# A linear-attention and mixture-of-experts layer: x loaded a second time in turned layout, and a new place for the normalisation of x1

## The chip, the cores and the metric

The kernel runs on one core of a Trainium2 chip. The metric is the time on the device in microseconds (us); less is better. TensorE is called PE here as in the profile (PEld is its weight load), VectorE is DVE, ScalarE is ACT, GpSimd is POOL and SyncE, which here only issues DMAs, is SP.

## The reference

x has 8 batches of 512 tokens with 256 features, in float32. One layer is two blocks, each with a residual and a layer norm:

```
q, k, v = x@Wq+bq, x@Wk+bk, x@Wv+bv         # 16 heads of 16 features
q, k = elu(q)+1, elu(k)+1
kv = sum over tokens of k v^T, per head and batch
attn = q @ kv;  gate = sigmoid(x@Wg+bg)
x1 = layernorm(x + (gate*attn)@Wo + bo)
weights, experts = top 4 of softmax(x1@gate_w.T), from the best 2 of 4 groups
y = sum over the 4 experts of weight * (silu(x1@w1)*(x1@w3))@w2
z = (silu(x1@ws1)*(x1@ws3))@ws2              # shared expert
out = layernorm(x1 + y + z)
```

## The kernel before

The program is written out by hand for each engine's queue; nothing plans it. It has four stages. First the attention of the eight batches, in a loop of batches (`batch(b, ...)` exists once for each engine). Then the shared expert for three batches. Then the routed experts in two waves of 48 blocks of 256 token rows each: the rows of x1 are sent by indirect DMAs of POOL into a table in HBM sorted by expert, SP loads blocks of it, PE turns and multiplies them, and SP stores the results. Last, POOL gathers the results and DVE adds them up and normalises, while PE does the shared expert for the other batches.

A product of float32 quality is made of three products of 16-bit halves: every operand is split in a high part by ACT (a copy to float16, `xt_hi`, `split_hi`) and a low part by DVE (a subtraction, `xt_lo`, `split_lo`).

In the attention of batch b, PE does in this order: `project_kv` of four token tiles (with `project_out(b - 1)` after the second), the transposes of the next batch's x (`transpose_x(x_in, ...)`), the two halves of q, the transposes of x1 of batch b - 1 (`transpose_x(x_all[...])`), the first half of the gate g, `sum_kv`, the second half of g, the routing products of batch b - 1 (`count_tokens`, `route`), and `attend(b)`. The transposes of x and of x1 go into the same two PSUM banks (`t_bank`).

ACT takes k and v out of PSUM (`take_kv`), makes the high half of the next x (L500), normalises x1 (L510), evaluates relu and exp of q (`q_parts`, L554 and L557), makes the high half of x1 (L505), splits two experts' weights (L516, L517) and evaluates the gate (L569). In ACT's batches 2 to 5 such a split also stands between the second and third `take_kv`.

DVE applies the gate (L686), finishes the routing of batch b - 2 (`routing_tail`), adds the residual (L718), takes the statistics (L691, L699), makes the low half of the next x (L671), adds the bias bo to the next x (`x_plus_bias`, L704, from `x_in` to `x_all`), finishes k (L913), splits weights (L709), finishes q (L919), makes the low half of x1 (L677), masks kv (L927, L930) and starts the routing of batch b - 1 (L730). Its queue, like the others, runs strictly in order. POOL makes from mean and variance four small instructions (L426 to L431), the last being the shift of the layer norm, which ACT waits for.

SP loads x of batch b into `x_in` (L262) once `x_plus_bias` of the batch before has read it, and the experts' weights into `stage` (L268, L270) once the split before is done. Between two loads of weights it writes, three times over, four blocks of zeros of 512 KB to the table in HBM (L292), and then loads x. At the start it issues the load of x of batch 0, the attention's weights, biases and constants, the shared expert's weights, and then waits.

Of the kernel before, what the change touches and what calls it, by code (L numbers as in the profile page):

```python
# [16 lines left out]
P = 128  # L17
# [15 lines left out]
def attention_and_experts(nc: bass.Bass, x, Wq, bq, Wk, bk, Wv, bv, Wg, bg, Wo, bo,  # L33
                          gate_w, w1, w2, w3, ws1, ws2, ws3, plan_consts, out):
# [36 lines left out]
    with ExitStack() as ctx:  # L71
# [11 lines left out]
        x_in = sb("x_in", [P, TT, D])  # L83
# [16 lines left out]
        eps = sb("eps", [P, TT])  # L100
# [102 lines left out]
        x_loaded, wa_loaded, small_loaded = sem("x_loaded"), sem("wa_loaded"), sem("small_loaded")  # L203
# [14 lines left out]
        x_transposed, xt_hi_ready, xt_lo_ready = sem("x_transposed"), sem("xt_hi_ready"), sem("xt_lo_ready")  # L218
# [9 lines left out]
        bn_ready, mv_ready, rstd_ready = sem("bn_ready"), sem("mv_ready"), sem("rstd_ready")  # L228
        x1_ready, x1_transposed, rstd_step = sem("x1_ready"), sem("x1_transposed"), sem("rstd_step")
# [30 lines left out]
        def _(sp):  # L260
            def load_x(b):
                sp.dma_start(x_in[:, :, :], x[b].rearrange("(p t) d -> p t d", p=P)).then_inc(x_loaded, 16)  # L262
# [9 lines left out]
            load_x(0)  # L272
# [9 lines left out]
            load_stage(0)  # L282

# [15 lines left out]
            def next_x(b):  # L299
                sp.wait_ge(x_biased, b)  # L300
                load_x(b)
# [97 lines left out]
        def _(pool):  # L399
# [5 lines left out]
            pool.memset(eps[:, :], LN_EPS).then_inc(const_ready, 1)  # L405
# [15 lines left out]
            pool.wait_ge(const_ready, 6)  # L421
# [71 lines left out]
        def _(act):  # L493
# [39 lines left out]
            def batch(b, prev, prev2, nxt, early=None, mid=None):  # L533
# [11 lines left out]
                if prev:  # L545
# [915 lines left out]
```

## Time and profile before

| what | us |
|---|---|
| median of 3 runs | 700.07 |
| the three runs | 700.07, 696.46, 704.74 |
| the profiled execution, its own time | 707.36 |
| span of that execution | 705.5 |
| PE busy | 527.1 (75%) |
| DVE busy | 427.4 (61%) |
| ACT busy | 300.1 (43%) |
| POOL busy | 290.1 (41%) |
| mean granted PE clock | 0.916 |

The span is from the first to the last instruction of the profiled execution. Busy time is summed over instructions, and PE's weight loads overlap its products. Attention takes the first 227 us of the span, the shared expert the time to 270, the two waves of experts that to about 600, and the rest is gathering, adding and the last shared products. A release named "remote" is one for which the profile shows no sender.

### The profile page before, as it was taken

To read this page: it belongs to the slowest core of one execution; us is meant where nothing else is said; L and a number is where in the kernel's file an instruction comes from. 1 tells how busy PE (TensorE), PEld (TensorE's weight loads), DVE (VectorE), ACT (ScalarE), POOL (GpSimd) and SP (SyncE) were. 2 spreads that over 40 slices of the span, in tenths; PEclk is the share of its full clock that TensorE was granted. 3 is DMA by queue.
4 is the path that set the end of the run, shared out by engine and by line. 5 is a ranking of instruction groups with operands and counts; after the bars stand their busy time and mean duration, and the time that the engine had idled before them with its cause. 6 is when DMAs were issued, how large, how long until landed. Compare 5 with 4: busy or idle time off the path is not lost.

```text
span 705.5 us, 13461 instructions
## 1 busy us (share of the span) xinstructions
PE 527.1 (75%) x3532; PEld 357.0 (51%) x3555; DVE 427.4 (61%) x1200; ACT 300.1 (43%) x659; POOL 290.1 (41%) x334
## 2 busy tenths in 40 slices
PE   1899887889897688789786688798888779665400
PEld 1355443555544357567574566576667566421300
DVE  2447783776864866666554444377757556652784
ACT  2536653436524343555454555356546445110100
POOL 1000126456446402454444200644446251777574
PEclk9999997899999899999999999899999989977755
DMA  7022428295451303767767766687787753333332
GB/s 202 13 75 76 156 90 284 82 304 209 177 185 68 103 18 106 239 204 230 232 228 259 238 223 216 180 235 233 211 261 231 223 181 134 105 120 89 94 114 99
DMA packets 64091, 118.63 MB, mean 168 GB/s; under 512 B 9760, under 2 KB 23088, under 8 KB 64048
## 3 DMA queue, kind: packets, MB, share of 16 engines
q1 hardware_dynamic: 51216, 84.55, 37.1%
q0 software_dynamic: 12288, 33.57, 15.1%
q8 instruction: 19, 0.31, 0.2%
q14 instruction: 24, 0.20, 0.1%
q10 hardware_dynamic: 544, 0.00, 0.0%
HBM read 55.17 MB, written 62.91 MB: 167 GB/s over the span
## 4 chain that ended last, share of the span: by engine, by line
PE 36%; DVE 19%; issue 15%; SPq 9%; another core or an unknown queue 6%; ACT 6%; DMA 5%; POOL 4%; ACTq 0%; DVEq 0%; POOLq 0%
PE t L1340 4%; PE h_even L1149 4%; PE h_even L1151 4%; PE h_odd L1149 3%; PE h_even L1150 3%; PE h_odd L1151 3%; PE h_odd L1150 3%; DVE x_all L1055 2%; SPq L327 2%; PE y L1186 2%; DMA kv<-expert_in 2%; SPq L330 1%; PE y L1373 1%; SPq L334 1%
## 5 line engine op out<-in xcount | busy, mean ns | idle before, releaser
L440 POOL DMA_INDIRECT expert_in<-x_all,slots x128 | 132.9, 1038 | 117.8 <-PE h_odd L1151 45.0
L452 POOL DMA_INDIRECT wa_stage<-expert_out,result_of x64 | 62.9, 983 | 35.3 <-issue 18.1
L1340 PE MATMUL t<-ident,kv 128*128 128x128 f32 x384 | 60.3, 280 | 19.4 <-DMA kv<-expert_in 15.0
L452 POOL DMA_INDIRECT q_fm<-expert_out,result_of x32 | 32.4, 1014 | 85.6 <-DMA expert_out<-q_exp 63.9
L426 POOL TENSOR_SCALAR neg_mean<-mv 128x4 f32<-128x4 f32 x16 | 4.6, 290 | 149.5 <-DVE mv L699 149.3
L1044 DVE TENSOR_TENSOR wa_lo<-bias_heads,wa_hi 128x256 bf16<-128x256 f32 x96 | 40.5, 422 | 41.3 <-ACT wa_hi L642 30.1
L1149 PE MATMUL h_even<-xsT_hi,we_hi 128*128 128x256 f16 x192 | 54.3, 283 | 10.7 <-issue 8.8
L1340 PEld LDWEIGHTS t<-ident,kv 128*128 128x128 f32 x384 | 45.3, 145 | 26.8 <-DMA kv<-expert_in 12.1
L1025 DVE TENSOR_TENSOR xsT_lo<-t,xsT_hi 128x512 bf16<-128x512 f32 x72 | 49.5, 688 | 11.6 <-ACT xsT_hi L617 5.9
L1150 PE MATMUL h_even<-xsT_lo,we_hi 128*128 128x256 bf16 x192 | 54.2, 282 | 2.5 <-issue 2.5
L1151 PE MATMUL h_even<-xsT_hi,we_lo 128*128 128x256 f16 x192 | 54.2, 282 | 1.4 <-issue 1.4
L617 ACT ACTIVATE xsT_hi<-t 128x512 f16<-128x512 f32 x72 | 42.0, 585 | 16.6 <-PE t L1340 12.8
L642 ACT ACTIVATE wa_hi<-bias_heads 128x256 f16<-128x256 f32 x96 | 39.7, 414 | 20.7 <-DVE bias_heads L1036 14.4
L1036 DVE TENSOR_TENSOR bias_heads<-h_odd,kv_heads 128x256 f32<-128x256 f32 x48 | 20.2, 420 | 41.8 <-ACT kv_heads L634 40.9
L1036 DVE TENSOR_TENSOR bias_heads<-h_even,kv_heads 128x256 f32<-128x256 f32 x48 | 20.1, 419 | 34.4 <-ACT kv_heads L634 30.9
L634 ACT ACTIVATE kv_heads<-h_odd 128x256 f32<-128x256 f32 x48 | 18.3, 381 | 52.8 <-remote 25.0
L1186 PE MATMUL y<-wo_sb,gated 128*128 128x256 f32 x128 | 33.3, 419 | 9.3 <-DVE gated L686 9.3
L452 POOL DMA_INDIRECT gate<-expert_out,result_of x32 | 30.5, 954 | 19.4 <-PE h_even L1151 10.0
L529 ACT ACTIVATE kv<-h_even 128x256 f32<-128x256 f32 x32 | 12.3, 386 | 58.3 <-PE h_even L1151 52.4
L634 ACT ACTIVATE kv_heads<-h_even 128x256 f32<-128x256 f32 x48 | 18.2, 380 | 43.8 <-PE h_even L1151 17.4
L1367 PE MATMUL y<-we_hi,wa_hi 128*128 x96 | 26.8, 279 | 12.6 <-issue 10.7
L624 ACT ACTIVATE k_exp<-y 128x512 f32<-128x512 f32 x48 | 28.7, 598 | 15.9 <-PE y L1373 14.3
(222 smaller groups left out, 1530.0 us busy)
## 6 DMA issues: line engine op xcount, KB each, us to landing
kv<-expert_in SPq DMA_DIRECT2D x96, 256.0 KB
expert_out<-k_exp SPq DMA_DIRECT2D x48, 256.0 KB
expert_out<-q_exp SPq DMA_DIRECT2D x48, 256.0 KB
expert_in<-wa_stage SPq DMA_DIRECT2D x16, 512.0 KB
expert_in<-wa_stage SPq DMA_DIRECT2D x32, 256.0 KB
stage<-in_L_ffn_w SPq DMA_DIRECT2D x48, 128.0 KB
x_in<-in_L_attn_x SPq DMA_DIRECT2D x8, 512.0 KB
out<-gated SPq DMA_DIRECT2D x8, 512.0 KB
```

The costliest lines, as they stand in the source:

```text
L440: pool.indirect_dma_start(xs_dram[b // WB], bass.IndirectOffsetOnAxis(ap=slots[:, b, t, j:j + 1], axis=0), x_all[:, b, t, :], None).then_i ...
L452: pool.indirect_dma_start(y_got[i][:, j, :], None, ys_dram[w], bass.IndirectOffsetOnAxis(ap=result_of[:, b, t, j:j + 1], axis=0)).then_inc ...
L617: act.activation(xsT_hi[r][:, :, :], t_bank[r % 2][:, :].rearrange("p (c n) -> p c n", c=KC), ACT.Copy).then_inc(xst_hi_ready, 1)
L642: act.activation(aT_hi[r % 2][:, :], a_pair, ACT.Copy).then_inc(at_hi_ready, 1)
L1025: dve.tensor_tensor(xsT_lo[r][:, :, :], t_bank[r % 2][:, :].rearrange("p (c n) -> p c n", c=KC), xsT_hi[r][:, :, :], ALU.subtract).then_in ...
L1036: dve.tensor_tensor(a_pair, h_banks[r % 2][0][:, 2 * P:], s_pair, ALU.mult).then_inc(pair_a_ready, 1)
L1044: dve.tensor_tensor(aT_lo[r % 2][:, :], a_pair, aT_hi[r % 2][:, :], ALU.subtract).then_inc(at_lo_ready, 1)
L1149: pe.matmul(dst, sta_hi, mov_hi, start=start, stop=False)
L1150: pe.matmul(dst, sta_hi, mov_lo, start=False, stop=False)
L1151: return pe.matmul(dst, sta_lo, mov_hi, start=False, stop=stop)
L1186: last = pe.matmul(y_bank[h][:, (t % 2) * D:(t % 2 + 1) * D], gated[:, c, t * P:(t + 1) * P], wo_sb[:, c, :], start=c == 0, stop=c == KC - 1)
L1340: last = pe.transpose(t_bank[r % 2][:, c * 2 * P + i * P:c * 2 * P + (i + 1) * P], xs[r][:, i, c * P:(c + 1) * P], ident[:, :])
```

## The change

A second copy of x is passed in as `x_turned`, with features before tokens, so that a DMA loads it just as the products want it. SP loads it into `x_in` (`load_xt`) once the low half of the batch before is made, and loads x itself straight into `x_all` (`load_x`); DVE adds bo there in place. The transposes of x on PE go, ACT and DVE read `x_in` in place of the PSUM banks, and PE's order becomes q, first half of g, transposes of x1, `sum_kv`. ACT normalises x1 between the two halves of `q_parts`, and evaluates the gate's first half before it takes the transposed x1. DVE makes the negative mean (for the first layer norm only) and variance plus epsilon; POOL is left with the power, and with the shift in the first layer norm only.

```diff
+            def load_xt(b):
+                sp.dma_start(x_in[:, :, :], x_turned[b].rearrange("(c p) s -> p c s", p=P)).then_inc(xt_loaded, 16)
+
             def load_x(b):
-                sp.dma_start(x_in[:, :, :], x[b].rearrange("(p t) d -> p t d", p=P)).then_inc(x_loaded, 16)
+                sp.dma_start(x_all[:, b, :, :], x[b].rearrange("(p t) d -> p t d", p=P)).then_inc(x_loaded[b], 16)
...
-            load_x(0)
+            load_xt(0)
...
             load_stage(0)
+            load_x(0)
...
             def next_x(b):
-                sp.wait_ge(x_biased, b)
+                sp.wait_ge(xt_lo_ready, KC * b)
+                load_xt(b)
                 load_x(b)
...
             def rstd_of(ln):
                 pool.wait_ge(mv_ready, ln + 1)
-                pool.tensor_scalar(neg_mean[:, :], mv[:, :, 0], -1.0, None, ALU.mult)
-                pool.tensor_tensor(var_eps[:, :], mv[:, :, 1], eps[:, :], ALU.add).then_inc(rstd_step, 1)
-                pool.wait_ge(rstd_step, 2 * ln + 1)
-                pool.tensor_tensor(rstd[:, :], var_eps[:, :], minus_half[:, :], ALU.pow).then_inc(rstd_step, 1)
-                pool.wait_ge(rstd_step, 2 * ln + 2)
-                pool.tensor_tensor(shift[:, :], neg_mean[:, :], rstd[:, :], ALU.mult).then_inc(rstd_ready, 1)
+                power = pool.tensor_tensor(rstd[:, :], var_eps[:, :], minus_half[:, :], ALU.pow)
+                if ln >= NB:
+                    power.then_inc(rstd_ready, 1)
+                else:
+                    power.then_inc(rstd_step, 1)
+                    pool.wait_ge(rstd_step, ln + 1)
+                    pool.tensor_tensor(shift[:, :], neg_mean[:, :], rstd[:, :], ALU.mult).then_inc(rstd_ready, 1)
...
             def xt_hi(b):
                 for c in range(KC):
-                    act.wait_ge(x_transposed, KC * b + c + 1)
-                    act.activation(xT_hi[:, c, b, :], t_bank[c][:, :], ACT.Copy).then_inc(xt_hi_ready, 1)
+                    if c == 0:
+                        act.wait_ge(xt_loaded, 16 * (b + 1))
+                    act.activation(xT_hi[:, c, b, :], x_in[:, c, :], ACT.Copy).then_inc(xt_hi_ready, 1)
...
-                if prev:
-                    normalize_x1(b - 1)
...
                 q_parts(0)
+                if prev:
+                    normalize_x1(b - 1)
                 q_parts(1)
+                gate_part(0)
                 if prev:
                     x1t_hi(b - 1)
                 if mid is not None:
                     split_hi(mid)
-                for c in range(KC):
-                    act.wait_ge(g_projected, KC * b + c + 1)
...
+                gate_part(1)
...
             def xt_lo(b):
                 for c in range(KC):
                     dve.wait_ge(xt_hi_ready, KC * b + c + 1)
-                    dve.tensor_tensor(xT_lo[:, c, b, :], t_bank[c][:, :], xT_hi[:, c, b, :],
+                    dve.tensor_tensor(xT_lo[:, c, b, :], x_in[:, c, :], xT_hi[:, c, b, :],
                                       ALU.subtract).then_inc(xt_lo_ready, 1)
...
-                last.then_inc(mv_ready, 1)
+                last.then_inc(moments_ready, 1)
+                dve.wait_ge(moments_ready, ln + 1)
+                if first:
+                    dve.tensor_scalar(neg_mean[:, :], mv[:, :, 0], -1.0, None, ALU.mult)
+                dve.tensor_scalar(var_eps[:, :], mv[:, :, 1], LN_EPS, None, ALU.add).then_inc(mv_ready, 1)
...
             def x_plus_bias(b):
-                dve.wait_ge(x_transposed, KC * (b + 1))
-                dve.tensor_tensor(x_all[:, b, :, :], x_in[:, :, :],
+                dve.wait_ge(x_loaded[b], 16)
+                dve.tensor_tensor(x_all[:, b, :, :], x_all[:, b, :, :],
                                   b_o[:, :].unsqueeze(1).to_broadcast([P, TT, D]), ALU.add).then_inc(x_biased, 1)
...
-                if nxt:
-                    transpose_x(x_in, x_transposed)
-                if prev:
-                    pe.wait_ge(gate_ready, KC * b)
-                project_features(b, 0, 2 * D, q_projected)
-                project_features(b, 1, 2 * D, q_projected)
-                if nxt:
-                    pe.wait_ge(xt_lo_ready, KC * (b + 2))
                 if prev:
                     pe.wait_ge(x1_ready, b)
                     transpose_x(x_all[:, b - 1, :, :], x1_transposed)
-                pe.wait_ge(q_exp_ready, KC * b + 1)
-                project_features(b, 0, 3 * D, g_projected)
                 sum_kv(b)
...
-            pe.wait_ge(x_loaded, 16)
-            transpose_x(x_in, x_transposed)
```

The first place is PE's queue in batch 1, from the end of `project_kv` on; h_odd holds q and then g, and only the rows with a wait are kept. Before:

```order
L1156 MATMUL t<-ident,x_in 128x128 [waits x_loaded]
...
L1149 MATMUL h_odd<-xT_hi,wa_hi 128x512 [waits gate_ready]
...
L1156 MATMUL t<-ident,x_all 128x128 [waits x1_ready,xt_lo_ready]
...
L1149 MATMUL h_odd<-xT_hi,wa_hi 128x512 [waits q_exp_ready]
...
L1195 MATMUL h_even<-kv 128x129 [waits k_ready]
```

And now:

```order
L1164 MATMUL h_odd<-xT_hi,wa_hi 128x512 [waits gate_ready]
...
L1164 MATMUL h_odd<-xT_hi,wa_hi 128x512 [waits q_exp_ready]
...
L1171 MATMUL t<-ident,x_all 128x128 [waits x1_ready]
...
L1210 MATMUL h_even<-kv 128x129 [waits k_ready]
```

The transposes of x_in are gone, and the wait for x1 stands behind g's first half, right ahead of `sum_kv`.

The second place is ACT's queue in batch 1, behind the last `take_kv`. Before:

```order
L500 ACTIVATE xT_hi<-t 128x512 [waits x_transposed] x2
L510 ACTIVATE x_all<-x_all,shift,rstd 128x256 [waits rstd_ready]
...
L554 ACTIVATE q_fm<-h_odd,b_q 128x512 [waits attended,q_projected,small_loaded]
L557 ACTIVATE q_exp<-h_odd,b_q 128x512 [waits q_ready]
L554 ACTIVATE q_fm<-h_odd,b_q 128x512 [waits attended,q_projected]
...
L505 ACTIVATE xT_hi<-t 128x512 [waits x1_transposed] x2
L516 ACTIVATE we_hi<-stage 128x768 [waits stage_loaded]
...
L569 ACTIVATE gate<-h_odd,half_b_g 128x512 [waits gated_ready,g_projected] x2
```

And now:

```order
L507 ACTIVATE xT_hi<-x_in 128x512 [waits xt_loaded]
...
L559 ACTIVATE q_fm<-h_odd,b_q 128x512 [waits attended,q_projected,small_loaded]
L562 ACTIVATE q_exp<-h_odd,b_q 128x512 [waits q_ready]
L517 ACTIVATE x_all<-x_all,shift,rstd 128x256 [waits rstd_ready]
...
L559 ACTIVATE q_fm<-h_odd,b_q 128x512 [waits attended,q_projected]
...
L569 ACTIVATE gate<-h_odd,half_b_g 128x512 [waits gated_ready,g_projected]
L512 ACTIVATE xT_hi<-t 128x512 [waits x1_transposed] x2
L523 ACTIVATE we_hi<-stage 128x768 [waits stage_loaded]
```

The normalisation is behind q's first half, and one gate instruction is ahead of the high half of x1.

The third place is SP's queue at the start, from the shared expert's last load on. Before:

```order
L270 DMA stage<-in_L_ffn_ws 128x256
L262 DMA x_in<-in_L_attn_x 128x1024 [waits x_biased]
L268 DMA stage<-in_L_ffn_w 128x2x128 [waits we_lo_ready]
L268 DMA stage<-in_L_ffn_w 128x2x128
L270 DMA stage<-in_L_ffn_w 128x256
```

And now:

```order
L274 DMA stage<-in_L_ffn_ws 128x256
L266 DMA x_all<-in_L_attn_x 128x1024
L263 DMA x_in<-in_x_turned 128x2x512 [waits xt_lo_ready]
L266 DMA x_all<-in_L_attn_x 128x1024
L272 DMA stage<-in_L_ffn_w 128x2x128 [waits we_lo_ready]
```

x of batch 0 is now loaded last of all that the start needs, and each later x is two loads where it was one; DVE's first `x_plus_bias` waits for x of batch 0.

## Rows read from the trace of the kernel before

**Rows 1.** By stretch: length, busy us (instructions) of PE, PEld, DVE, ACT, POOL, clock, DMA, GB/s.

```profile
137.00:164.00 27.00, 23.51 (x131) 13.75 (x131) 19.57 (x67) 13.50 (x31) 15.64 (x17) 0.94 0.64 215
...
270.00:630.00 360.00, 292.56 (x2260) 223.21 (x2262) 212.14 (x529) 174.77 (x395) 153.42 (x165) 0.96 0.66 207
```

**Rows 2.** Groups of instructions by line, 10 to 240 us: busy, mean ns | idle before.

```profile
L671 DVE TENSOR_TENSOR xT_lo<-t,xT_hi 128x512 bf16<-128x512 f32 x14 | 9.0, 686 | 17.4 <-ACT xT_hi L500 17.4
...
L1156 PE MATMUL t<-ident,x_all 128*128 128x128 f32 x56 | 8.1, 291 | 12.4 <-ACT x_all L510 11.8 <-issue 0.6
...
L1156 PE MATMUL t<-ident,x_in 128*128 128x128 f32 x56 | 7.3, 273 | 0.0
```

**Rows 3.** The same view, 230 to 262 us.

```profile
L990 DVE TENSOR_TENSOR a_lo<-x_in,a_hi 128x512 bf16<-128x512 f32 x4 | 2.8, 692 | 2.8 <-ACT a_hi L602 2.8
```

**Rows 4.** Waits, 10 to 240 us: us in total, times, longest us.

```profile
ACT we_hi L516 <- DMA stage<-in_L_ffn_w: 31.8, 7, 7.4
...
DVE logits L730 <- remote: 19.8, 5, 8.9
...
PE t L1156 <- ACT x_all L510: 11.8, 6, 4.1
```

**Rows 5.** Timeline of PE, batch 1: start, us, line, operation.

```profile
49.80 1.04 PE L1156 MATMUL t<-ident,x_in 128*128 128x128 f32 x8
...
50.68 0.38 PE L1149 MATMUL h_odd<-xT_hi,wa_hi 128*128 128x512 f16 x1
```

**Rows 6.** Timeline of VectorE and then of PE, batch 5.

```profile
163.78 1.29 DVE L671 TENSOR_TENSOR xT_lo<-t,xT_hi 128x512 bf16<-128x512 f32 x2 [2.46 <-ACT xT_hi L500]
...
171.78 0.62 DVE L930 SCALAR_TENSOR_TENSOR kv_heads<-bias_heads,h_even,kv_heads 128x128 f32<-128x128 f32 x2
...
172.50 1.96 PE L1203 MATMUL y<-q_fm,kv_heads 128*128 128x512 f32 x4
```

**Rows 7.** Timeline of PE, batches 2 and 7.

```profile
78.48 1.64 PE L1156 MATMUL t<-ident,x_all 128*128 128x128 f32 x8 [2.87 <-ACT x_all L510]
...
79.92 0.63 PE L1149 MATMUL h_odd<-xT_hi,wa_hi 128*128 128x512 f16 x1
...
82.36 1.84 PE L1195 MATMUL h_even<-kv 128*128 128x129 f32 x15
...
217.75 1.09 PE L1156 MATMUL t<-ident,x_all 128*128 128x128 f32 x8 [4.09 <-ACT x_all L510]
```

**Rows 8.** Timeline of GpSimd and VectorE, batches 2 and 4.

```profile
74.27 1.04 POOL L429 TENSOR_TENSOR rstd<-var_eps,minus_half 128x4 f32<-128x4 f32 x1
...
74.85 1.22 DVE L704 TENSOR_TENSOR x_all<-x_in,b_o 128x1024 f32<-128x1024 f32 x1
...
75.39 0.73 POOL L431 TENSOR_TENSOR shift<-neg_mean,rstd 128x4 f32<-128x4 f32 x1
...
139.98 2.49 POOL L440 DMA_INDIRECT expert_in<-x_all,slots  x1 [0.30 <-issue]
```

**Rows 9.** Timeline of SyncE queue and ScalarE, batches 4 and 5.

```profile
149.24 1.14 SPq L262 DMA_DIRECT2D x_in<-in_L_attn_x  x1
...
152.10 1.70 SPq L268 DMA_DIRECT2D stage<-in_L_ffn_w  x2
...
160.05 0.84 ACT L516 ACTIVATE we_hi<-stage 128x768 f16<-128x768 f32 x1 [6.96 <-DMA stage<-in_L_ffn_w]
```

**Rows 10.** Start: timeline of SyncE and VectorE, then one window as in Rows 1.

```profile
11.78 0.47 SPq L270 DMA_DIRECT2D stage<-in_L_ffn_ws  x1
...
14.49 1.22 DVE L704 TENSOR_TENSOR x_all<-x_in,b_o 128x1024 f32<-128x1024 f32 x1 [6.29 <-DMA plan_sb<-in_plan_consts]
...
17.00:18.00 1.00, 0.00 (x0) 0.00 (x0) 1.00 (x2) 0.00 (x0) 0.00 (x0) 1.00 0.94 340
```

**Rows 11.** Timeline of GpSimd, end.

```profile
699.16 0.23 POOL L426 TENSOR_SCALAR neg_mean<-mv 128x4 f32<-128x4 f32 x1 [4.34 <-DVE mv L699]
...
700.74 0.20 POOL L431 TENSOR_TENSOR shift<-neg_mean,rstd 128x4 f32<-128x4 f32 x1
```

More of the change, by code:

```diff
@@ L200, in attention_and_experts @@
         last_count_bank = h_banks[0][1]
-        x_loaded, wa_loaded, small_loaded = sem("x_loaded"), sem("wa_loaded"), sem("small_loaded")
+        xt_loaded, wa_loaded, small_loaded = sem("xt_loaded"), sem("wa_loaded"), sem("small_loaded")
+        x_loaded = [sem(f"x_loaded{b}") for b in range(NB)]
         stage_loaded, out_stored = sem("stage_loaded"), sem("out_stored")
@@ L557, in q_parts, with gate_part @@
                     act.activation(q_exp[:, c, :], qg_bank[c][:, :], ACT.Exp, bias=b_q[:, c:c + 1]).then_inc(q_exp_ready, 1)
+                def gate_part(c):
+                    act.wait_ge(g_projected, KC * b + c + 1)
+                    if prev:
+                        act.wait_ge(gated_ready, KC * b)
+                    act.activation(gate[:, c, :], qg_bank[c][:, :], ACT.Tanh, bias=half_b_g[:, c:c + 1], scale=0.5).then_inc(gate_ready, 1)
                 q_parts(0)
+                if prev:
+                    normalize_x1(b - 1)
                 q_parts(1)
+                gate_part(0)
                 if prev:
@@ L564, in batch @@
                     split_hi(mid)
-                for c in range(KC):
-                    act.wait_ge(g_projected, KC * b + c + 1)
-                    if prev:
-                        act.wait_ge(gated_ready, KC * b)
-                    act.activation(gate[:, c, :], qg_bank[c][:, :], ACT.Tanh, bias=half_b_g[:, c:c + 1], scale=0.5).then_inc(gate_ready, 1)
+                gate_part(1)
             xt_hi(0)
@@ L686, in apply_gate, with norm_stats @@
                     dve.scalar_tensor_tensor(gated[:, c, :], gate[:, c, :], 1.0, y_bank[c][:, :], ALU.add, ALU.mult).then_inc(gated_ready, 1)
-            def norm_stats(rows, ln):
+            def norm_stats(rows, ln, first=False):
                 for t in range(TT):
@@ L1277, in _ @@
             pe.wait_ge(count_consts_ready, 2)
-            batch(0, False, False, True)
-            batch(1, True, False, True)
-            for b in range(2, 5):
-                batch(b, True, True, True)
-            batch(5, True, True, True)
-            batch(6, True, True, True)
-            batch(NB - 1, True, True, False)
+            for b in range(NB):
+                batch(b, b > 0, b > 1)
             def up(g, n, par):
@@ L1439, in _plan_constants, with _turned @@
     return np.concatenate(rows, axis=1).astype(np.float32)
+def _turned(x):
+    batches, tokens, features = x.shape
+    return x.reshape(batches, P, tokens // P, features).transpose(0, 3, 2, 1).reshape(batches, features, tokens)
 def kernel(**inputs):
@@ L1450 @@
     experts = inputs["L0_ffn_gate_w"].shape[0]
-    sources = dict(inputs, plan_consts=_plan_constants(_np, tokens_sent // P, experts))
-    for name in _INS + ["plan_consts"]:
+    sources = dict(inputs, plan_consts=_plan_constants(_np, tokens_sent // P, experts),
+                   x_turned=_turned(inputs["L0_attn_x"]))
+    for name in _INS + ["plan_consts", "x_turned"]:
         a = _np.ascontiguousarray(sources[name])
```

34 lines of the change are left out of this document (18 added, 16 removed).

## The prediction

> **What bounds the kernel now.** I read the busy time by stretch first, then the groups by line, then the waits of the attention, and last the timelines of single batches, because the change touches only attention (to 227 us), the start, and the layer norm at the end. The two waves of experts are PE work at full load, 292.56 of 360 us busy [rows 1], in loops that wait for each other and for nothing with a date of its own; what attention gains or loses should come out of them unchanged.
>
> In attention PE looks like the bound, but it is so only in part. In batch 4's stretch it is busy 23.5 of 27 us [rows 1]. Three other things hold it. x1 comes late: PE waits 11.8 us in six waits [rows 4]. The experts' weights come late: ACT waits 31.8 us in seven waits for them [rows 4], and behind ACT stand the eviction of k and v and the gate. And DVE's queue is full: in batch 5 it runs without a gap from the low half of x (163.78) to the masked kv (ends at 172.40), and `attend` starts at 172.50 [rows 6]. That last row is the one to keep in mind: PE had nothing to do with when it started. DVE then waits at L730 for a release that the profile cannot name, 19.8 us in five waits, the longest 8.9 [rows 4].
>
> **The transposes of x.** Eight matmuls a batch, 56 in seven batches, 273 ns each but overlapped [rows 2]: they hold PE from 49.80 to 50.68, 0.88 us [rows 5], 6.2 us in seven batches. The set for batch 0 lies ahead of loads that are waited for anyway. Are they on the path? The low half of x waits for ACT's high half, 17.4 us in all [rows 2], which stands behind `take_kv` of the last tile, and that ends later than the transposes of the first half. So DVE's chain starts where it did, and where DVE's chain ends the batch (0, 4, 5) PE's gain is idle time. In batches 1 and 6, x1 is nearly on time, and ACT's new order takes back what PE wins: the normalisation starts behind q's first half, 1.2 us later, x1's transposes with it, then its high half behind one more gate instruction. I take **0** for these five batches; bounds: −0.88 each (−4.4) and +0.5 each (+2.5). Reading x from SBUF changes nothing: DVE's subtraction took 686 ns from PSUM and 692 ns from SBUF [rows 2, 3].
>
> **x1 late, batches 2, 3 and 7.** Here x1 sets the time. In batch 2 x1's transposes start at 78.48 after 2.87 us of idleness, and g's first half, six matmuls, takes 79.92 to 82.36 at the half clock [rows 7]; at full speed it would be 1.2. In the changed order those six matmuls are done while PE waits, so 2.4 us leave the path. Against that, part of the half clock moves on to `sum_kv` behind it (about +0.6 of 1.8 us), and x1 itself gets no earlier. I take **−1.8** for batch 2, by rows 7. Batch 3 wins the same at `attend`, but the next thing is late too: the gate of batch 3 stands behind a weights load that is issued in DVE's order after the low half of x, the bias and k, and that order is no faster. So batch 3's win is not counted on its own. Batch 7 has the longest wait, 4.09 us [rows 7], and no weights to load: 2.5 gained, 0.9 given back to the half clock, **−1.6**. Bounds of the two terms together: 0 and −7.
>
> **The layer norm's arithmetic.** POOL loses the two instructions ahead of the power: 699.16 to 699.63 at the end, 0.47 us, and the shift behind it, 0.20 us [rows 11]. DVE gains a wait and one small instruction (0.25). So about 0.45 us for each norm on the path; two are, the last two batches' at the end: **−0.9**, bounds −0.4 and −2. In attention POOL's 0.47 is DVE's 0.35, nothing.
>
> There the trace warns of something: the shift took 0.73 us at 75.39 and not the 0.20 of 700.74, and it ended when DVE's addition of two SBUF operands (74.85, 1.22 us) ended; likewise an indirect DMA beside the weights' split took 2.49 us [rows 8, 11]. The subtraction L671 now reads two SBUF operands, and it runs as POOL's power is released. I put +0.5 us in batches 2 and 3 for it, inside the terms above. The Trainium skill, page "SBUF — State Buffer", section "Who interferes with whom", has this as a rule against the change: a DVE instruction with two SBUF inputs and a GpSimd one that reads SBUF lock each other out for a whole instruction. Rows 8 agree.
>
> **The second load, in the attention.** Every batch moves 512 KB more. The late load is that for weights issued behind the zeros and x: x is issued at 149.24, the weights at 152.10, and they are there at 160.05, ACT having idled 6.96 us [rows 9]. All are in one queue. 512 KB took about 1.5 us at 340 GB/s [rows 10], so weights behind them come 1.5 us later. That is on the path once, before batch 5, where ACT's evictions then run without a gap; before batch 3 and 4 there is slack of a us or so, which the x1 gain eats. **+1.5**, bounds 0 and +3.
>
> **The start.** DVE's first bias addition ran at 14.49, released by the constants [rows 10], and behind it in DVE's queue stand the low halves of the attention's weights, for which PE waits. It now waits for x of batch 0, issued after 11.78 + 0.47 = 12.25. The loads ahead are drained about 15; 512 KB at 340 GB/s [rows 10] bring it to about 16.3: **+1.8**. Bounds: +0.5, and +4.8 if it shares the engines with batch 1's two loads that are issued at once behind it (1.5 MB, 4.5 us).
>
> **Sum.** −1.8 − 1.6 − 0.9 + 1.5 + 1.8 = −1.0. The profiled execution took 707.36 (span 705.5), 7.3 us more than the median, and would be 706.4; I lay the terms on the median: 700.07 − 1.0 = **699.0**.
>
> **Rivals.**
>
> 1. PE is the bound after all. Then 6.2 us of transposes go, x1's waits shrink by what g covers (1.3 us at most of each, 5.9 in six waits), and the half clock behind three of them goes (3.6). With start and end: −6.2 − 5.9 − 3.6 + 1.8 − 0.9 = −14.8, 685. For it: PE's busy share; against: rows 6 and the 31.8 us for weights. 0.18.
> 2. The 8.9 us wait at L730 is an accident of one batch: the other four average (19.8 − 8.9)/4 = 2.7. If the new order moves the batch out of it, 6 us more are gained, if the timed runs before had it too: 693. 0.12.
> 3. Slower: that same wait comes back in more batches. It lies in batch 3, where PE also starved while zeros, x and weights went through at once, and it ended when they had. The bursts are now 512 KB longer and PE is a little earlier in them. It decides when a burst still runs as the routing products end. Two batches more with 8.9 for 2.7 to 3.4 are +11: 710. 0.12.
> 4. The start at its upper bound, the rest as forecast: 702. 0.07.
> 5. The lock between DVE and POOL costs a full instruction more in each late norm (1.2 us in three batches): 702.6. By the skill's rule alone it could be so, by rows 8 only half an instruction was lost. 0.05.
>
> The forecast has 0.46.
>
> **Chances.** About 1%, 7 us, is what a measurement here tells from no change: faster is under 693.1, slower over 707.1. Faster: all of rival 1, half of 2, and a tenth of the forecast's bounds, 0.29. Slower: rival 3 and the upper tails of the forecast and of rivals 4 and 5, 0.16. The rest, 0.55. The range, 685 to 708, has rival 1 at its edge and leaves out rival 3.
>
> **What would show it.** Right: PE's first projection begins near 21.3, not 19.45, released by DVE; `attend` of batches 1, 4, 5 and 6 follows DVE's masked kv as before; the transposes of x1 in batches 2, 3 and 7 start no earlier but `sum_kv` follows them at once; ACT's wait for weights grows. Wrong: batches of 22 us, PE busy throughout (rival 1); a wait at L745, the old L730, of more than 8 us in two batches (rival 3); a gain that lies in the waves of experts, which I hold to be untouched.

## The result, and the profile after

The changed kernel took 710.15 us (median of 4, 709.44 to 711.09), the kernel before 699.12 on the same chip (median of 4, 696.46 to 704.74): ratio 1.0125, 95% interval [1.0075, 1.0174]. It is slower, and outside the range of the forecast. On other chips the same two kernels compare otherwise (0.9932 and 1.001, below), and that difference is the heart of this case. A ratio is taken from the runs within 1.5% of the fastest of their kernel, a median from all of them.

The two executions whose traces are read here are closer to each other than the medians: spans of 705.5 us before and 707.7 after. That of before took 707.36, 8 us more than the median of four.

By stretch the changed kernel looks like before (the view and stretches of [rows 1]):

```profile
137.00:164.00 27.00, 22.71 (x124) 12.62 (x121) 18.14 (x66) 11.92 (x29) 15.40 (x15) 0.94 0.69 234
270.00:630.00 360.00, 295.47 (x2278) 225.94 (x2279) 215.41 (x551) 174.62 (x396) 146.73 (x149) 0.95 0.64 206
```

The experts cost TensorE (PE) 295 us for 293. The waits of the attention, 10 to 240 us, answer to [rows 4]:

```profile
ACT we_hi L523 <- DMA stage<-in_L_ffn_w: 38.6, 7, 9.9
DVE logits L745 <- remote: 29.6, 5, 10.3
```

ScalarE (ACT) waits 6.8 us more for weights, and VectorE (DVE) 9.8 us more at L745, the old L730, for a release that the profile cannot name: 6.3 us for 2.1 in batch 6 and 10.3 for 2.0 in batch 7, against 6.9 for 8.9 in batch 3. Where the longest of these waits lies is seen in the timeline of all engines behind batch 7's last products:

```profile
225.05 0.64 DVE L945 SCALAR_TENSOR_TENSOR kv_heads<-bias_heads,h_even,kv_heads 128x128 f32<-128x128 f32 x2
...
225.81 0.18 PE L1227 MATMUL t<-gwT_both,xT_lo 128*128 128x32 f16 x1
...
225.84 1.96 PE L1218 MATMUL y<-q_fm,kv_heads 128*128 128x512 f32 x4
...
230.49 0.38 PE L1166 MATMUL h_even<-xT_hi,we_lo 128*128 128x512 f16 x1
...
232.97 0.96 POOL L446 DMA_INDIRECT expert_in<-x_all,slots  x1 [0.30 <-issue]
236.00 0.29 DVE L745 TENSOR_REDUCE logits<-t 128x64 f32<-128x128 f32 x1 [10.30 <-remote]
...
237.87 1.29 DVE L697 SCALAR_TENSOR_TENSOR gated<-gate,y 128x512 f32<-128x512 f32 x2
...
239.21 0.79 PE L1201 MATMUL y<-wo_sb,gated 128*128 128x256 f32 x1 [8.35 <-DVE gated L697]
```

The last routing product, whose increment L745 waits for, is over at 225.99. VectorE starts at 236.00, and TensorE, which has gone on to 230.87, then stands for 8.35 us. The records of semaphore updates in the trace say what "remote" is: logits_ready counts up at 235.97, though its product ended at 225.99, and within a quarter of a us behind it come the increments of both attention products (226.94 and 227.80) and of two shared products (229.10, 230.87). **By the trace the work was done; TensorE's increments were held back, and these five were let go together**, two to three us behind the last DMA_INDIRECT that GpSimd (POOL) issued in a row of thirteen. Two others were let go earlier, in the middle of that row: the gate's second half, done at 225.39, counted at 227.41, and a routing sum, done at 225.58, counted at 230.27.

The kernel before had GpSimd in a row of seven there, from 224.56 to 233.11, and waited far less:

```profile
227.43 0.29 DVE L730 TENSOR_REDUCE logits<-t 128x64 f32<-128x128 f32 x1 [2.02 <-remote]
```

Its last routing product was done at 225.63 and counted at 227.40, while the row went on. So a row of DMA_INDIRECT does not tell by itself how long an increment is held; what does is open.

### The profile page after: what moved, and what is told of

Same layout as the page of the kernel before. It is cut to its first block, busy times and chain, and to the rows that moved or that the text cites. A ratio compares the mean times of both kernels' runs of the same rounds, so it can differ in the third digit from the quotient of the medians.

```text
span 707.7 us, 13336 instructions
## 1 busy us (share of the span) xinstructions
PE 526.5 (74%) x3490; PEld 352.6 (50%) x3491; DVE 430.8 (61%) x1224; ACT 299.3 (42%) x659; POOL 282.8 (40%) x293
## 4 chain that ended last, share of the span: by engine, by line
PE 39%; DVE 18%; issue 13%; SPq 8%; another core or an unknown queue 7%; ACT 5%; DMA 5%; POOL 4%; DVEq 0%; ACTq 0%; POOLq 0%
PE h_even L1164 5%; PE t L1342 5%; PE h_even L1166 4%; PE h_even L1165 4%; PE y L1201 3%; PE h_odd L1164 3%; PE h_odd L1166 3%; PE h_odd L1165 2%; DVE x_all L1070 2%; SPq L333 2%; DMA kv<-expert_in 1%; PE y L1369 1%; PE y L1375 1%; DVE we_lo L724 1%
## 5 line engine op out<-in xcount | busy, mean ns | idle before, releaser
L431 POOL TENSOR_TENSOR rstd<-var_eps,minus_half 128x4 f32<-128x4 f32 x16 | 17.4, 1088 | 160.4 <-DVE var_eps L715 160.3
L1342 PEld LDWEIGHTS t<-ident,kv 128*128 128x128 f32 x384 | 45.9, 145 | 26.4 <-DMA kv<-expert_in 11.9
L1201 PE MATMUL y<-wo_sb,gated 128*128 128x256 f32 x128 | 38.8, 470 | 18.3 <-DVE gated L697 18.3
L653 ACT ACTIVATE wa_hi<-bias_heads 128x256 f16<-128x256 f32 x96 | 39.7, 414 | 24.5 <-DVE bias_heads L1051 19.8
L628 ACT ACTIVATE xsT_hi<-t 128x512 f16<-128x512 f32 x72 | 42.1, 586 | 14.4 <-PE t L1342 12.5
L1201 PEld LDWEIGHTS y<-wo_sb,gated 128*128 128x128 f32 x128 | 30.3, 242 | 27.6 <-DVE gated L697 21.7
```

The source lines that it names most:

```text
L628: act.activation(xsT_hi[r][:, :, :], t_bank[r % 2][:, :].rearrange("p (c n) -> p c n", c=KC), ACT.Copy).then_inc(xst_hi_ready, 1)
L653: act.activation(aT_hi[r % 2][:, :], a_pair, ACT.Copy).then_inc(at_hi_ready, 1)
L1201: last = pe.matmul(y_bank[h][:, (t % 2) * D:(t % 2 + 1) * D], gated[:, c, t * P:(t + 1) * P], wo_sb[:, c, :], start=c == 0, stop=c == KC - 1)
L1342: last = pe.transpose(t_bank[r % 2][:, c * 2 * P + i * P:c * 2 * P + (i + 1) * P], xs[r][:, i, c * P:(c + 1) * P], ident[:, :])
```

## How many increments come late, and on which chips

For each TensorE instruction with an increment I took the first update of its semaphore from its end on, left out those with none within 30 us, and counted those over 1 us late. "Time" is the median, "ratio" is to the kernel before on the same chip. The traces of the slower chips also lack records (below), and where the update of an increment is missing, a later one stands in its place. The number in brackets counts the late ones with an update of their own, that is one that belongs to no later product; a missing record does not explain these.

| run | chip | time / before | ratio [95%] | late, 20-100 us | late, 100-235 us (own update) | DVE logits <- remote, us |
|---|---|---|---|---|---|---|
| before, first trace | first | 699.12 | | 0 of 58 | 31 of 88 (24) | 19.8 |
| after, first trace | first | 710.15 / 699.12 | 1.0125 [1.0075, 1.0174] | 0 of 50 | 28 of 81 (24) | 29.6 |
| before_again | 1 | 645.73 / 647.68 | | 0 of 57 | 2 of 94 (0) | none |
| pace_after | 1 | 641.16 / 647.68 | 0.9894 [0.9861, 0.9928] | 0 of 49 | 0 of 88 (0) | none |
| pace_before | 1 | 646.23 / 647.68 | 0.9975 [0.9951, 0.9999] | 0 of 58 | 1 of 93 (0) | none |
| order_back | 1 | 654.67 / 647.68 | 1.0105 [1.0071, 1.0139] | 0 of 48 | 1 of 81 (0) | none |
| after_again | 8 | 643.94 / 648.36 | 0.9932 [0.9907, 0.9957] | 0 of 49 | 0 of 87 (0) | none |
| x_early | 8 | 637.00 / 648.36 | 0.9809 [0.9768, 0.9851] | 0 of 50 | 1 of 85 (0) | none |
| x_early_bias | 8 | 631.45 / 648.36 | 0.9725 [0.9683, 0.9767] | 0 of 53 | 2 of 87 (0) | none |
| x_early_bias_pace | 8 | 632.44 / 648.36 | 0.9753 [0.9720, 0.9787] | 0 of 53 | 1 of 90 (0) | none |
| after_third | 11 | 714.75 / 710.94 | 1.0010 [0.9981, 1.0040] | 0 of 49 | 29 of 78 (25) | 31.8 |
| pace_after_2 | 11 | 708.58 / 710.94 | 0.9943 [0.9916, 0.9970] | 0 of 50 | 20 of 85 (10) | none |
| moments_back | 11 | 724.71 / 710.94 | 1.0153 [1.0097, 1.0208] | 0 of 48 | 26 of 75 (23) | 26.1 |
| order_before | 11 | 707.03 / 710.94 | 0.9939 [0.9887, 0.9990] | 0 of 60 | 27 of 82 (22) | 25.9 |
| moments_back_2 | 11 | 720.04 / 709.23 | 1.0064 [0.9993, 1.0136] | 0 of 48 | 31 of 80 (26) | 32.5 |
| order_before_2 | 11 | 704.05 / 709.23 | 0.9945 [0.9906, 0.9983] | 0 of 60 | 29 of 86 (22) | 22.0 |
| x_early_bias_2 | 11 | 706.60 / 709.23 | 0.9999 [0.9952, 1.0046] | 0 of 53 | 30 of 83 (23) | 19.1 |
| x_early_bias_pace_2 | 11 | 694.45 / 709.23 | 0.9807 [0.9739, 0.9875] | 0 of 53 | 22 of 86 (13) | 2.1 |
| moments_back_3 | 2 | 650.28 / 647.53 | 1.0052 [1.0020, 1.0084] | 0 of 49 | 2 of 88 (0) | none |
| pace_before_2 | 2 | 646.52 / 647.53 | 0.9990 [0.9966, 1.0014] | 0 of 59 | 0 of 92 (0) | none |

There are two kinds of chip: chips 1, 2 and 8, here called clear, on which the kernel before takes 648 us and no increment is late with an update of its own, and the first chip and chip 11, here called holding, on which it takes 699 to 711 and a third of the increments are late. The number of the first chip is not on record; it may be chip 11. None is late before 100 us anywhere, and the first DMA_INDIRECT of the first chip's traces is issued at 102.5. Times from different chips are compared by their ratios. The batch tables further down put one trace of each kernel side by side from three clear chips, on which the kernel before has medians of 647.5 to 648.4.

## The experiments

**Chip 1.** before_again is the kernel before. pace_after and pace_before move GpSimd's dispatch. The edit is shown here in short, three rows being SPREAD:

```
for b in range(3, NB):
-    pool.wait_ge(kv_projected, TT * b + 2); dispatch(3 rows)
-    if b > 3: rstd_of(b - 1)
-    dispatch(3 rows); pool.wait_ge(q_projected, ...); dispatch(3 rows)
-    pool.wait_ge(kv_summed, b + 1); dispatch(3 rows)
+    if b > 3:
+        pool.wait_ge(attended, KC * b); dispatch(6 rows); rstd_of(b - 1)
+    dispatch(6 rows)
+pool.wait_ge(attended, KC * NB)
```

order_back takes the changed kernel and puts `normalize_x1` ahead of `q_parts(0)`, x1's transposes ahead of `project_features(b, 0, 3 * D, ...)`, and `x1t_hi` ahead of both gate parts again.

> The kernel before, once more, for its trace. Held-increment theory (TensorE's semaphore increments come late while GpSimd issues a row of DMA_INDIRECT, and VectorE's L730 waits for them): L730 waits of some 15 to 22 us in all, each ending within 3 us behind the last DMA_INDIRECT of a group, the largest in batch 3. Accident theory (the 8.9 us in the first trace was a disturbance, and L730 costs under 8 us in a run near 698): then the sum is below 8 us here if the span is near 696.

> The changed kernel with GpSimd's dispatch moved: six DMA_INDIRECT behind each batch's attention products, then the layer norm's pow, six more, and then it waits for the next batch's attention products, so that it issues none in the 3 to 5 us in which TensorE finishes the routing and attention products. Held-increment theory: the 29.6 us of L745 <- remote fall below 6 us, and the time goes from 710 to 685 to 695 (the 8 us of batch 7 whole, and parts of batches 3, 5 and 6). Transfer theory (VectorE waits because SP's bursts of weights, zeros and the second x load hold the queues): L745 stays at 20 us or more, since the bursts are unchanged, and the time stays at 705 to 712.

> The same move in the kernel before. Held-increment theory: L730 <- remote falls from 19.8 us to under 6, time 685 to 695; the change's own effect, with the stall gone from both, is then the difference to the paced changed kernel, which my terms put at -3 to +3 us. Transfer theory: no change, 696 to 705.

> The changed kernel with the order of before on ScalarE (x1 normalised ahead of q's first half) and TensorE (transposes of x1 ahead of the gate's first half), the turned x kept. If the turned x itself (the 4.2 MB more, the earlier batches) costs the time: 708 to 712. If the moved x1 costs it, by where it puts the batches against GpSimd's groups: 697 to 703. By my terms (cover of x1 worth 3.4 us in batches 2 and 7): 712 to 714.

The chip was a clear one, which I had not foreseen: no kernel waited for remote, so the pacing had nothing to remove and the tests of it said nothing of the held increments. What they gave is a trace of before without the disturbance. order_back: without the new order the changed kernel is 1% slower than before. The three expectations were times for a chip like the first; set against the changed kernel they asked for −2 to +2 us, −13 to −7, or, by my own terms, +2 to +4. Against the changed kernel on chip 8 it is 1.7% (11 us) slower: the sign of the last, three times its size.

**Chip 8.** x_early takes `load_x(b)` out of `next_x` and issues it for batches 1 to 7 right behind `next_x(1)`; x_early_bias also moves `x_plus_bias(0)` from ahead of the weights' low halves to just ahead of `batch(0, ...)`.

```
 def next_x(b):
     sp.wait_ge(xt_lo_ready, KC * b); load_xt(b)
-    load_x(b)
 next_x(1)
+for b in range(1, NB):
+    load_x(b)
 next_stage(1)
```

> The changed kernel again, beside the others of this call. Traffic theory (the second 0.5 MB load per batch delays the stage loads behind GpSimd's and SP's bursts in batches 3 to 5, and the start is 3.2 us later): ratio to before 1.005 to 1.013, the wait of the early split (L523 <- DMA stage) 6 to 10 us in batches 4 and 5, and the intervals between the attention products of batches 3 to 5 about 30 us where before has 25 to 27. Held-increment theory: ratio 1.012 only where L745 shows waits from remote; without them the changed kernel is at 0.995 or less.

> The changed kernel with the second load of x for batches 1 to 7 issued in one row right behind the start's loads, in the stretch of 13 to 40 us where the queues are idle; the turned loads stay where they are. The bytes are the same. Traffic theory: the intervals of batches 3 to 5 fall to before's 25 to 27 us, the time falls by 6 to 9 us against the changed kernel. Layout theory (what costs is the turned x itself: its 2 KB runs, x_in held until VectorE's xT_lo): no more than 2 us gained, since the turned loads keep their places in the bursts. The first batch may lose up to 1 us to the row of loads.

> The same, and the bias of batch 0 is added to x just ahead of VectorE's batch 0 and not ahead of the weights' lower halves, so that VectorE does not wait for the last load of the start. My start term, mis-sized: the first product then comes 3 to 5 us earlier than in x_early (18 to 20 us for 23.1), and the time falls by as much. If the small loads' end at 14.5 us holds TensorE just as well: under 1 us.

> The same, with GpSimd's dispatch paced behind the attention products. Held-increment theory: on a chip whose L745 shows waits from remote it gains 8 to 20 us more against x_early_bias; on one that shows none, under 2 us either way. In all, against the kernel before: 0.975 to 0.985.

On a clear chip the change is 0.7% faster, as the held-increment theory asked (0.995 or less) and the traffic theory (1.005 to 1.013) did not. x_early gains 1.2% of before's time on top (7 us between the medians), within what traffic was expected to give and far above the 2 us of the layout theory; the late bias another 0.8%, 5.5 us; pacing nothing.

**Chip 11.** moments_back computes `neg_mean` and `var_eps` on GpSimd again; order_before puts the new order alone into the kernel before.

```
 power of rstd_of(ln), moments_back:
+    pool.tensor_scalar(neg_mean, mv[:, :, 0], -1.0, None, ALU.mult)
+    pool.tensor_tensor(var_eps, mv[:, :, 1], eps, ALU.add)
 norm_moments(ln), moments_back:
-    dve.tensor_scalar(neg_mean, ...); dve.tensor_scalar(var_eps, ...)
```

> The changed kernel, beside the others of this call. Chip theory (the first chip holds the engines' semaphore increments back from the first DMA_INDIRECT on, the second and third do not): ratio near 0.993 where the trace shows no wait from remote at L745, near 1.012 where it does. Chance theory (the first comparison was an outlier): 0.993 on any chip.

> The changed kernel with mean and variance plus epsilon computed on GpSimd again, as before; turned x and order kept. My term gives the move 0.9 us, all in the tail of the last layer norms, so 1 us slower than the changed kernel. If the 3.6 us by which the stretch from the last expert store to the end is shorter than before's comes from it: 3 to 4 us slower. If a part of the attention batches' gain comes from it too (shift a third of a us earlier in each): up to 6 us slower.

> The kernel before with the new order alone (ScalarE normalises x1 behind q's first half, TensorE transposes x1 behind the gate's first half), x loaded once and transposed on TensorE. If the order is worth the 10 us by which order_back ended its attention later than the changed kernel: 638 to 641 on a chip where before has 648, so ratio 0.985. If the order only pays once TensorE has no transposes of the next x (they hold t0 and t1 until VectorE's xT_lo): within 2 us of before.

> The paced changed kernel once more. Held-increment theory: equal to after_third within 2 us where no wait from remote shows (0.989 against 0.993 so far); 8 us or more faster than it where L745 waits for remote.

The chip was a holding one. The waits of after_third and of x_early_bias_2, over 10 to 300 us, in this order:

```profile
DVE logits L745 <- remote: 31.8, 5, 10.4
ACT gate L569 <- remote: 9.5, 2, 5.3
```

```profile
DVE logits L746 <- remote: 19.1, 5, 5.9
```

In pace_after_2 there is no such row for VectorE's logits, though 20 of its increments are still late, 10 with an update of their own: they are late where VectorE's logits do not wait. In x_early_bias_pace_2 one wait is left:

```profile
DVE logits L743 <- remote: 2.1, 1, 2.1
```

The projection behind batch 7's attention starts at 242.5 in after_third and at 226.8 in pace_after_2. The time follows less than that: 0.9943 for 1.001, or 6 us between the medians, where 8 had been expected. The traced execution of after_third, 725.12, was the longest of its eleven (709.02 to 725.12), so the 15.7 us between the two starts are no measure of a usual run.

after_third also missed its own expectation: with 31.8 us of waits from remote it was to be near 1.012 and is 1.001, and near 0.993 by the chance theory, which its interval excludes. moments_back is 1.4% slower than after_third, 10 us, where at most 6 had been allowed. order_before gains 0.6%, between its two expectations (0.985, or no more than 2 us).

**Chip 11 again, and chip 2** (moments_back_3 and pace_before_2). The same kernels again.

> The changed kernel with mean and variance plus epsilon on GpSimd again. Where no wait from remote shows: 3 to 5 us slower than the changed kernel's 0.993 of before, so a ratio of 0.998 to 1.001, if the tail's gain is this move's; 0.994 to 0.995 if my 0.9 us stands. Where L745 waits for remote: 1.01 to 1.02 as in the run before.

> The kernel before with the new order alone. Where no wait from remote shows: 0.985 if the order carries the batches' gain without the turned x, 0.997 to 1.003 if it needs the transposes of the next x gone. The run on the chip with held increments gave 0.9939.

> The changed kernel with the early row of x loads and the late bias of batch 0. Without held increments 0.9725 as before; with them, its batches still run into GpSimd's groups: L745 waits 20 to 32 us for remote, ratio 0.98 to 0.99.

> The same with GpSimd's dispatch behind the attention products. Without held increments 0.975 as before; with them L745 shows no wait from remote and it is 5 us or more faster than x_early_bias_2: 0.970 to 0.978.

> The changed kernel with mean and variance plus epsilon on GpSimd again. Where no wait from remote shows: the stretch from the last expert store to the end takes 104 us again for 100.4, and the ratio is 0.998 to 1.001 for the changed kernel's 0.993; with my 0.9 us it would be 0.9945. Where L742 waits for remote: 1.006 to 1.015.

> The kernel before with GpSimd's dispatch behind the attention products. Where no wait from remote shows: 0.9975 as before. With held increments: its L730 waits (19.8 us in the first trace) fall below 4 us, ratio 0.985 to 0.992.

This settles that pacing gains on a holding chip. On the clear chip it moved x_early_bias from 0.9725 to 0.9753, on the holding one from 0.9999 to 0.9807, 12 us between the medians; the ten runs of one kernel (699.30 to 713.04) and the four of the other (692.93 to 697.83) do not overlap. Both missed the expected ratio (0.98 to 0.99, and 0.970 to 0.978), the gain of 5 us or more came. x_early_bias lost there all that it had won on chip 8, as far as its interval can tell (0.9952 to 1.0046). Whether pacing helps the kernel before on a holding chip was not seen: pace_before_2 ran on a clear one. So no run separates what the held increments cost the change from what they cost the kernel before. moments_back_3, at 1.0052, is slower than the 0.998 to 1.001 expected; moments_back_2, 1.0064 with an interval from 0.9993, says little.

That GpSimd's row of DMAs alone does not hold anything back, a clear chip shows; the changed kernel, chip 8, batch 7, timeline of all engines:

```profile
218.25 0.96 POOL L446 DMA_INDIRECT expert_in<-x_all,slots  x1 [0.30 <-issue]
218.94 0.62 DVE L945 SCALAR_TENSOR_TENSOR kv_heads<-bias_heads,h_even,kv_heads 128x128 f32<-128x128 f32 x2
...
219.78 1.96 PE L1218 MATMUL y<-q_fm,kv_heads 128*128 128x512 f32 x4
219.97 0.29 DVE L745 TENSOR_REDUCE logits<-t 128x64 f32<-128x128 f32 x1 [0.41 <-PE t L1227]
...
220.78 0.96 POOL L446 DMA_INDIRECT expert_in<-x_all,slots  x1 [0.30 <-issue]
```

L745 follows the routing products at once, named, in the middle of the same row of DMAs.

## Why the prediction was wrong, step by step

**The step that failed is the one on L730.** The sum left its wait as it was (0), and rival 3 gave its return 0.12. The runs show it to be a wait for TensorE's increments, held back on some chips while GpSimd issues DMA_INDIRECTs; it grew from 19.8 to 29.6 us. The rival's time, 710, came true to the digit, and part of its reasoning did: the waits grew by 9.8 us where it said 11, in batches 6 and 7. That the time did is partly luck, since the two traced spans differ by 2.2 us only and batch 7's output projection (`project_out`) starts 8.6 us later (239.21 for 230.64). And its mechanism was wrong. It tied the wait to SyncE's bursts of zeros, x and weights, and its condition was a burst still running as the routing products end. At 226 to 236 us no such burst runs (SyncE issues nothing there, the DMA engines are 0.26 busy), and pacing GpSimd with the bursts unchanged took the wait away. What the runs point to is this: on a chip that holds increments, GpSimd is in a row of DMA_INDIRECT as the routing products end. In the kernel before, GpSimd had paused 1.4 us for kv_summed (L1195) in batch 7 and issued again from 224.56; changed, it ran from 217.49 to 233.93 without a pause. That this pause is why before waited 2.0 us and not 10.3 was not tested. What is shown is that pacing removes the wait on a holding chip and that the release is late there. That this is the whole of the first 1.25% is an inference: the changed kernel alone has given 1.0125 and 1.001 on holding chips, and x_early_bias 0.9999 where a clear chip gave 0.9725.

**The sum itself** is read on clear chips (before_again and order_back on chip 1, after_again and x_early on 8, moments_back_3 on 2; one trace each), from the starts of the attention products in batches 0 to 7 (first row of L1203 or L1218 in each) and two ends:

| | 0 | 1 | 2 | 3 | 4 | 5 | 6 | 7 | last expert store | end of span |
|---|---|---|---|---|---|---|---|---|---|---|
| before_again | 38.5 | 60.8 | 87.1 | 111.8 | 139.2 | 164.3 | 190.5 | 217.2 | 540.0 | 644.0 |
| after_again | 42.1 | 64.2 | 87.6 | 113.2 | 145.1 | 172.9 | 196.5 | 219.8 | 541.2 | 641.6 |
| order_back | 41.7 | 64.0 | 90.4 | 114.5 | 145.4 | 175.2 | 202.6 | 230.0 | 551.4 | 652.1 |
| x_early | 40.7 | 62.7 | 86.2 | 111.8 | 140.1 | 167.0 | 192.3 | 217.4 | 538.0 | 638.7 |
| moments_back_3 | 41.4 | 63.5 | 87.8 | 112.8 | 143.4 | 171.5 | 197.6 | 221.8 | 544.7 | 648.1 |

- **The start**, taken at +1.8, was +3.6 (42.1 for 38.5). The mechanism held; the changed kernel's first trace, timeline of VectorE and TensorE, beside [rows 10]:

```profile
18.22 1.23 DVE L719 TENSOR_TENSOR x_all<-x_all,b_o 128x1024 f32<-128x1024 f32 x1 [10.59 <-DMA x_all<-in_L_attn_x]
19.36 2.35 DVE L963 TENSOR_TENSOR wa_lo<-wa_stage,wa_hi 128x1024 bf16<-128x1024 f32 x2
...
23.14 0.59 PE L1164 MATMUL h_even<-wa_hi,xT_hi 128*128 128x512 f16 x1 [8.31 <-DVE ones L979]
```

  The bias starts 3.7 us later than 14.49, not 1.8, and the first product comes at 23.14, where I had asked for 21.3. That x shares the engines with batch 1's two loads, as in my upper bound, is an inference: x_early has six more loads right behind and starts its first product no later, at 22.80. x_early_bias, whose VectorE does not wait there, starts its first attention products at 35.3, 5.4 earlier than x_early.
- **x1 behind g**, taken at −1.8 in batch 2 and −1.6 in batch 7: batch 2 took 23.4 for 26.3 (−2.9), batch 7 23.3 for 26.7 (−3.4), and batch 6, which I had put at 0, 23.6 for 26.2 (−2.6). With the order undone these three take 26.4, 27.4 and 27.4. So 0 for the batches where "ACT's new order takes back what PE wins" was wrong for batch 6, right for batch 1 (22.1 for 22.3). In all, undoing the order costs 10.2 us at batch 7 and 1.7% of the time, across two clear chips. The order alone, in the kernel before, gives 0.994 on the holding chip twice; on a clear one it did not run.
- **The second load**, taken at +1.5: batches 4 and 5 took 31.9 and 27.8 for 27.4 and 25.1, +7.2 together. Batch 3, whose gain I had not counted, took 25.6 for 24.7. x_early, the same bytes outside the bursts, took 28.3 and 26.9 in batches 4 and 5, still 2.7 more than before together. ScalarE's wait for weights ahead of batch 4's last evictions, timelines of before_again, after_again and x_early:

```profile
125.35 0.84 ACT L516 ACTIVATE we_hi<-stage 128x768 f32 x1 [7.06 <-DMA stage<-in_L_ffn_w]
```

```profile
130.85 0.84 ACT L523 ACTIVATE we_hi<-stage 128x768 f32 x1 [11.04 <-DMA stage<-in_L_ffn_w]
```

```profile
127.22 0.84 ACT L524 ACTIVATE we_hi<-stage 128x768 f32 x1 [8.85 <-DMA stage<-in_L_ffn_w]
```

  I had counted 512 KB once and one batch. By the program a late stage makes the next stage's issue late as well, since SyncE waits for VectorE's low half of the one before; that this is the rest was not tested. x_early gave back 3.5 us in batches 6 and 7 (25.3 and 25.1 for 23.6 and 23.3); why is open. Its profiled run was the slowest of its four, 640.41.
- **The layer norm**, taken at −0.9: from the last store of the experts to the end, 100.4 for 104.0, −3.6, and 103.4 with the move undone. The undone move costs 1.2% in all (1.0052 for 0.9932), 6.5 us by the spans: 2.0 by batch 7, 1.5 to the last store, 3.0 behind it. I had counted two norms at the very end. The last norm, timelines of GpSimd, moments_back_3 and then after_again, beside [rows 11]:

```profile
634.61 0.94 POOL L459 DMA_INDIRECT wa_stage<-expert_out,result_of  x1 [0.30 <-issue]
635.58 0.26 POOL L433 TENSOR_SCALAR neg_mean<-mv 128x4 f32<-128x4 f32 x1
635.79 0.21 POOL L434 TENSOR_TENSOR var_eps<-mv,eps 128x4 f32<-128x4 f32 x1
636.08 1.04 POOL L436 TENSOR_TENSOR rstd<-var_eps,minus_half 128x4 f32<-128x4 f32 x1
637.21 0.20 POOL L438 TENSOR_TENSOR shift<-neg_mean,rstd 128x4 f32<-128x4 f32 x1
```

```profile
629.50 0.95 POOL L458 DMA_INDIRECT wa_stage<-expert_out,result_of  x1 [0.30 <-issue]
630.46 1.05 POOL L431 TENSOR_TENSOR rstd<-var_eps,minus_half 128x4 f32<-128x4 f32 x1
636.05 1.01 POOL L431 TENSOR_TENSOR rstd<-var_eps,minus_half 128x4 f32<-128x4 f32 x1 [4.54 <-DVE var_eps L715]
```

  Per norm the move saves what I said, 0.5 us ahead of the power and 0.2 behind it. I take it to be paid in more norms than two, since in the second wave GpSimd's gathers stand behind each norm in its queue, but which of them are on the path I did not test.
- **The lock** of VectorE and GpSimd (rival 5) shows in GpSimd, and not in VectorE, whose subtraction took 688 ns from two SBUF operands for 686 from PSUM. GpSimd's power took at most 1.06 us in before_again; in after_again it took 1.38, 1.41 and 1.94 us in batches 2, 6 and 7. In before_again the negative mean or the shift was longer in its place. Batch 7 of before_again and then, beside VectorE, of after_again:

```profile
204.73 1.10 POOL L426 TENSOR_SCALAR neg_mean<-mv 128x4 f32<-128x4 f32 x1 [5.05 <-DVE mv L699]
206.07 1.04 POOL L429 TENSOR_TENSOR rstd<-var_eps,minus_half 128x4 f32<-128x4 f32 x1
```

```profile
210.54 1.22 DVE L928 SCALAR_TENSOR_TENSOR kv<-k_exp,kv 128x1024 f32<-128x1024 f32 x1
210.72 1.94 POOL L431 TENSOR_TENSOR rstd<-var_eps,minus_half 128x4 f32<-128x4 f32 x1 [4.73 <-DVE var_eps L715]
```

  From GpSimd's first instruction of the norm to the end of the shift it is 2.31 us for 2.33 in batch 2, 2.30 for 2.27 in batch 6 and 2.22 for 2.66 in batch 7: in two of these three the lock takes back what the two instructions fewer give. The +0.5 us that the sum had for it in batch 2 was right (0.3 in the power, 0.1 in the shift), and the batch gained all the same. In batch 7 it is the k instruction that stands beside the power, not the subtraction that I had named.
- **Rival 1**, TensorE the bound, was wrong: batches 3 to 5 stayed at 25.6 to 31.9 us. **Rival 2**, the accident, was half right: on a clear chip the wait is not there at all, but on a holding one it is there in every unpaced trace.

My sum, −1.0, beside −4.4 us between the medians on chip 8 (−2.4 between the two spans of the table), was near only because errors of opposite sign met. In the table the start is +3.6 (taken 1.8), batches 3 to 5 are +8.1 (taken 1.5), batches 2, 6 and 7 −8.9 (taken −3.4), the end −3.6 (taken −0.9), and batch 1 with the experts −1.6 (taken 0): together −2.4.

## A version that beats both

x_early_bias_pace, the changed kernel with x loaded in one row at the start, the first bias behind the weights and the dispatch paced, is 2.5% faster than before on a clear chip and 1.9% on a holding one. x_early_bias, as good on the clear chip, gained nothing on the holding one that its interval can tell.

## What to carry to other kernels

A wait whose releaser the profile cannot name is no constant of the kernel: look up when the semaphore was counted up and when its work ended, and what a third engine was doing, before it goes into a sum as 0. Where increments come late as here, put rows of indirect DMAs where no other engine waits for an increment, and move a load that has no date out of the burst that others wait for. And compare on more than one chip where the answer is 1%: here it went from −0.7% to +1.25%.

## What the runs showed of the hardware

On the holding chips increments of TensorE's semaphores reached their waiters late, by the longest wait at L745 up to 10 us, and only while GpSimd issued DMA_INDIRECTs. None was late in the 80 us ahead of the first one, at 102.5 us, though from 85 to 95 us the DMA engines were 0.80 busy in the kernel before and 0.99 in the changed one. Between 280 and 560 us 100 of 247 were late in the kernel before on the first chip (90 with an update of their own), none of 278 on chip 1. And none was late in the longest pause of GpSimd's DMAs, from 395 to 441 us of that trace: 0 of 40. It is the same in all ten traces of holding chips: from 1 us behind the last DMA_INDIRECT on, no increment is late in any pause over 12 us.

**The holding chips are slower only where GpSimd issues DMA_INDIRECTs, too.** Up to the attention products of batch 2 the kernel before needs 86.0 us on the first chip and 87.1 on chip 1. Of the 152 stores of the experts' results, from the first to the 73rd it takes 126.8 us for 106.7, from there to the 89th, with no DMA_INDIRECT beside them, 34.9 for 34.6, and to the 145th 134.1 for 113.8. The windows of the first two stretches, first chip and then chip 1:

```profile
278.90:405.70 126.80, 100.30 (x814) 78.55 (x813) 70.26 (x174) 65.12 (x150) 56.83 (x58) 0.99 0.72 231
405.70:440.60 34.90, 28.70 (x241) 22.73 (x239) 15.93 (x32) 18.84 (x43) 0.00 (x0) 1.00 0.66 219
```

```profile
269.20:375.90 106.70, 95.59 (x821) 79.19 (x820) 72.42 (x174) 66.60 (x150) 56.34 (x58) 1.00 0.85 276
375.90:410.50 34.60, 28.66 (x240) 22.68 (x238) 16.45 (x32) 18.81 (x43) 0.00 (x0) 1.00 0.68 218
```

The granted clock is 0.99 and 1.00 in the slow stretch, so it is not the clock. That the late increments are what makes these chips 8% slower fits all of this but was not tested, and what holds them back is open.

The records of the holding chips have gaps as well: the first trace of before has 456 updates for ScalarE's 542 increments and 690 for VectorE's 845, before_again 556 and 882. Every run on record, traced or timed, comes with a span and a granted clock of its own; none shows the program without any recording, so that the recording takes part in the delay is not excluded.
